# Exponents of a gated attention cell as fp32r products: Z in two parts instead of three, the mask's product first, rows of a parity on their own partitions

## The reference, cut to what matters

```python
ig, fg = gates(q, k, v)                      # 8 heads each
log_f = jax.nn.log_sigmoid(fg)
cs = jnp.cumsum(log_f, axis=1)
log_D = where(tril, cs[:, :, None] - cs[:, None, :], -inf) + ig[:, None, :]
max_log_D = jnp.max(log_D, axis=-1, keepdims=True)
D_mat = jnp.exp(log_D - max_log_D)
C = (qh @ kh.T / sqrt(32)) * D_mat
normalizer = maximum(abs(C.sum(-1)), exp(-max_log_D))
h = (C / (normalizer + 1e-6)) @ vh           # then a norm over 256 features, and x = x + h
```

## Time and profile before

| | |
|---|---|
| device time, 3 runs | median 572.49 us (571.02 to 572.50) |
| profiled execution | 568.18 us, span of the engines 566.5 us |
| PE busy | 547.5 us (97%) |
| DVE busy | 326.7 us (58%) |
| ACT busy | 230.2 us (41%) |
| stage A | about 25.2 to 118.7 us of the span |

### The profile page before, as it was taken

The page is one execution under the profiler, slowest core; times in us unless marked ns, Lnnn a source line. Parts: engine busy times, 40 slices in busy tenths (PEclk is TensorE's granted clock), DMA queues, the critical chain, the costliest instruction groups (busy, mean ns, idle before and its releaser), DMA issues.

```text
span 566.5 us, 8464 instructions
## 1 busy us (share of the span) xinstructions
PE 547.5 (97%) x2773; PEld 447.2 (79%) x2773; DVE 326.7 (58%) x799; ACT 230.2 (41%) x436; POOL 71.2 (13%) x105
## 2 busy tenths in 40 slices
PE   7798998999999999899999999999999999999997
PEld 5566576679888888778888878888878889788887
DVE  6677789768877779773353463434552444542333
ACT  2344545647878844362121361122351122441111
POOL 5232324111412323100000000000000000000000
PEclk9998999999999999999999999999999999999999
DMA  7685537334986999200000100000100000000001
GB/s 206 161 199 175 99 105 185 91 118 169 363 303 204 198 318 229 78 1 0 1 0 1 37 2 1 0 1 0 37 1 1 1 1 19 20 1 0 1 0 39
DMA packets 59296, 47.69 MB, mean 84 GB/s; under 512 B 37278, under 2 KB 50590, under 8 KB 58852
## 3 DMA queue, kind: packets, MB, share of 16 engines
q1 hardware_dynamic: 54264, 30.39, 20.1%
q0 software_dynamic: 4848, 16.78, 9.1%
q10 hardware_dynamic: 148, 0.04, 0.0%
HBM read 40.58 MB, written 2.10 MB: 75 GB/s over the span
## 4 chain that ended last, share of the span: by engine, by line
PE 58%; issue 7%; POOL 2%; DVE 1%; POOLq 0%; DVEq 0%
PE ps L914 57%; POOL rstd L445 1%; POOL h L551 1%; PE ps L584 0%; PE ps L878 0%; DVE qr L1527 0%; DVE x L1515 0%; DVE xn L1275 0%; DVE alT L1554 0%; DVE xT L1282 0%; POOL w L540 0%; POOLq L551 0%; POOL w L542 0%; PE ps L869 0%; DVE ot L1607 0%
## 5 line engine op out<-in xcount | busy, mean ns | idle before, releaser
L914 PE MATMUL ps<-hBt,h 128*128 128x512 f32 x512 | 117.5, 390 | 0.0
L914 PE MATMUL ps<-hA,h 128*128 128x512 f32 x512 | 117.3, 390 | 0.0
L1238 ACT ACTIVATE h<-ps,scol 128x512 f32<-128x512 f32 x64 | 44.2, 690 | 175.3 <-PE ps L914 175.2
L914 PEld LDWEIGHTS ps<-hA,h 128*128 128x128 f32 x512 | 95.9, 188 | 20.4 <-DVE hA L1581 0.6
L914 PEld LDWEIGHTS ps<-hBt,h 128*128 128x128 f32 x512 | 95.8, 188 | 20.3 <-DVE hBt L1581 0.6
L914 PE MATMUL ps<-xT,w 128*128 128x512 f32 x256 | 61.7, 396 | 1.0 <-DVE xT L1282 1.0
L914 PEld LDWEIGHTS ps<-xT,w 128*128 128x128 f32 x256 | 46.2, 188 | 15.0 <-issue 6.0
L1599 DVE CAST hBt<-h 128x512 fp32r<-128x512 f32 x32 | 13.7, 427 | 73.7 <-ACT h L1238 73.7
L1599 DVE CAST hA<-h 128x512 fp32r<-128x512 f32 x32 | 13.7, 427 | 70.0 <-ACT h L1238 70.0
L445 POOL TENSOR_TENSOR rstd<-ve,mhalf 128x4 f32<-128x4 f32 x16 | 16.7, 1041 | 262.9 <-DVE ve L1270 262.9
L1221 ACT ACTIVATE silD<-ps,scol 128x512 f32<-128x512 f32 x32 | 22.1, 689 | 45.2 <-PE ps L914 45.2
(11 more groups left out here) (174 smaller groups left out, 877.2 us busy)
## 6 DMA issues: line engine op xcount, KB each, us to landing
looked<-w_all_in SPq DMA_DIRECT2D x16, 704.0 KB, 5.6
h<-w_all_in POOLq DMA_DIRECT2D x16, 512.0 KB, 6.5
V<-ctx_in SPq DMA_DIRECT2D x32, 128.0 KB, 3.4
Qb<-xT SPq DMA_DIRECT2D x64, 64.0 KB, 2.1
w<-w_all_in POOLq DMA_DIRECT2D x3, 1024.0 KB, 7.7
x<-x_in SPq DMA_DIRECT2D x4, 512.0 KB, 4.2
kstA<-ctxT_in SPq DMA_DIRECT2D x4, 512.0 KB, 5.4
kstC<-ctxT_in SPq DMA_DIRECT2D x4, 512.0 KB, 5.8
```

The source lines that it names most:

```text
L914: last = mm(o, a, b, start=(k == 0 and p == 0), stop=(k == n_k - 1 and p == 1))
L1238: fn(h32[:, m % 2, :], ps[:, 2 + m % 4, :], ACT.Gelu, scale=scol[:, L + 1, m:m + 1])\
```

## The change

Z is split into two parts of fp32r in place of three of bf16. `gate_c` has two DVE operations for four, `move_rows` four DMAs for six (now of 4-byte elements, 16 KB instead of 8 KB each). `Rr` and `Lr` have 2 + 8 = 10 rows for 15; the rows of even groups lie on partitions 0 to 9, those of odd groups on partitions 32 to 41. The mask and the identity are fp32r as well; the mask is kept once (128 columns) and read four times over. In `expo` the mask's product comes first, then the rows' product. For the first batch of a group both mask products come before the wait for z_moved. A batch's two expo come one after the other, then its two qk. The ones rows and the mask are loaded by POOL (five DMAs that convert from bf16) and not by SP.

```diff
+ZP = 2
+RZ = ZP + ZP * Q
+RB = 32
-MOVES = 16 * 6
+MOVES = 16 * 2 * ZP
...
-        Rr = place(a3, "Rr", [RA, 2, Q, 2, Q, S], BF16)
-        Lr = place(a3, "Lr", [RA, 2, 2, Q, S], BF16)
+        Rr = place(a3, "Rr", [RB + RZ, Q, 2, Q, S], F32R)
+        Lr = place(a3, "Lr", [RB + RZ, 2, Q, S], F32R)
...
         def move_rows(sp, u):
-            for part in range(3):
-                sp.dma_start(Rr[part:part + 1, u, :, :, :, :], zp[:, part, 0, :]).then_inc(s["z_moved"], 16)
-                sp.dma_start(Lr[3 + part * Q:3 + part * Q + Q, u, :, :, :], zp[:, part, 1, :])\
-                    .then_inc(s["z_moved"], 16)
+            for part in range(ZP):
+                sp.dma_start(row_of(u, part), zp[:, part, 0, :].bitcast(F32)).then_inc(s["z_moved"], 16)
+                sp.dma_start(columns_of(u, part), zp[:, part, 1, :].bitcast(F32)).then_inc(s["z_moved"], 16)
...
+            def causal(quad):
+
+                mm(ps[:, EX + quad, :], idr[:, :], tri_all, start=True, stop=False)
+
             def expo(g, u, k):
                 q, quad = k // 2, k % 2
                 n = UN * g + k
                 if k == 0:
+                    for a in range(2):
+                        pe.wait_ge(s["d_ready"], n + a + 1)
+                        causal(a)
                     pe.wait_ge(s["z_moved"], MOVES * (g + 1))
-                    pe.wait_ge(s["d_ready"], n + 1)
-                mm(ps[:, EX + quad, :], Lr[:, u, quad, q, :], Rr[:, u, :, quad, q, :],
-                   start=True, stop=False)
-                mm(ps[:, EX + quad, :], idb[:, :], tri[:, :, :], start=False, stop=True)\
-                    .then_inc(s["expo_done"], 1)
+                elif k > 1:
+                    if quad == 1:
+                        pe.wait_ge(s["d_ready"], n + 1)
+                    causal(quad)
+                rows = slice(RB * u, RB * u + RZ)
+                mm(ps[:, EX + quad, :], Lr[rows, quad, q, :], Rr[rows, :, quad, q, :],
+                   start=False, stop=True).then_inc(s["expo_done"], 1)
...
-            pe.wait_ge(s["consts"], CONSTS)
+            pe.wait_ge(s["rows_ld"], ROWS)
...
                         for k in (2 * q, 2 * q + 1):
                             expo(g, u, k)
+                        for k in (2 * q, 2 * q + 1):
                             qk(g, u, k)
...
                 ch.step(v.tensor_copy(zp[:, 0, :, :], Z[:, :, :]))
                 ch.settle()
-                ch.step(v.tensor_tensor(zr[:, :, :], Z[:, :, :], zp[:, 0, :, :], ALU.subtract))
-                ch.settle()
-                ch.step(v.tensor_copy(zp[:, 1, :, :], zr[:, :, :]))
-                ch.settle()
-                v.tensor_tensor(zp[:, 2, :, :], zr[:, :, :], zp[:, 1, :, :], ALU.subtract).then_inc(s["z_ready"], 1)
+                v.tensor_tensor(zp[:, 1, :, :], Z[:, :, :], zp[:, 0, :, :], ALU.subtract).then_inc(s["z_ready"], 1)
```

More of the change, by code:

```diff
@@ L45 @@
 EPS = 1e-6
-CONSTS = 16 * 10
+A2 = 6
+CONSTS = 16 * 5
+ROWS = 16 * 5
 W_ALL = 2 * KD * HD + MD * D + 2 * MD * HD
@@ L128, in two_layers @@
         idf = place(base, "idf", [P, P], F32)
-        idb = place(base, "idb", [P, P], BF16)
-        tri = place(base, "tri", [P, Q, S], BF16)
+        idr = place(base, "idr", [P, P], F32R)
+        tri = place(base, "tri", [P, S], F32R)
         lns = place(base, "lns", [P, D], F32)
@@ L273, in _ @@
             sp.dma_start(gb[:, :], gb_in).then_inc(s["consts"], 16)
-            for u in range(2):
-                sp.dma_start(Rr[3:RA, u, :, :, :, :], ones_rows_in[3:RA]).then_inc(s["consts"], 16)
-                sp.dma_start(Lr[0:3, u, :, :, :], ones_rows_in[0:3, 0]).then_inc(s["consts"], 16)
-            sp.dma_start(tri[:, :, :], tri_in).then_inc(s["consts"], 16)
             sp.dma_start(x[:, Q:2 * Q, :], x_in[Q:2 * Q].rearrange("b s d -> s b d")).then_inc(s["x_second"], 16)
@@ L325, in _ @@
                     .then_inc(s["x_rest"], 16)
-            for part in range(3):
+            for part in range(ZP):
                 part_made(sp, part)
-                sp.dma_start(Rr[part:part + 1, 0, :, :, :, :], zp[:, part, 0, :]).then_inc(s["z_moved"], 16)
+                sp.dma_start(row_of(0, part), zp[:, part, 0, :].bitcast(F32)).then_inc(s["z_moved"], 16)
             queries_in(0, 0, 1)
@@ L460, in _ @@
                 .then_inc(s["gw_lo"], 1)
+            pool.dma_start(tri[:, :], tri_in[:, 0, :]).then_inc(s["rows_ld"], 16)
+            for u in range(2):
+                pool.dma_start(Rr[RB * u + ZP:RB * u + RZ, :, :, :, :], ones_rows_in[3:3 + ZP * Q]).then_inc(s["rows_ld"], 16)
+                pool.dma_start(Lr[RB * u:RB * u + ZP, :, :, :], ones_rows_in[0:ZP, 0]).then_inc(s["rows_ld"], 16)
             def k_lo(n, kst, u):
@@ L640, in qk @@
                 three(ps[:, QK + quad, :], lambda p: kT[:, u, p, quad, q * S:(q + 1) * S],
-                      lambda p: Qb[:, q % 2, p, quad, :, :], True, True,
-                      (lambda: pe.wait_ge(s["d_ready"], n + 2)) if quad == 0 else None).then_inc(s["qk_done"], 1)
+                      lambda p: Qb[:, q % 2, p, quad, :, :], True, True).then_inc(s["qk_done"], 1)
             def pv(b, par, nth, q, next_unit=None):
@@ L674, in _ @@
             pe.wait_ge(s["gw_lo"], 2)
-            pe.wait_ge(s["idb_ready"], 1)
+            pe.wait_ge(s["idr_ready"], 1)
             gates(0, 0, ctx_first=True)
@@ L1097, in _ @@
             floor_part(0)
-            for part in range(3):
+            for part in range(ZP):
                 part_made(act, part)
-                act.dma_start(Lr[3 + part * Q:3 + part * Q + Q, 0, :, :, :], zp[:, part, 1, :])\
-                    .then_inc(s["z_moved"], 16)
+                act.dma_start(columns_of(0, part), zp[:, part, 1, :].bitcast(F32)).then_inc(s["z_moved"], 16)
             with act.Fori(0, 2) as i:
```

42 lines of the change are left out of this document (24 added, 18 removed).

## The result

The changed kernel takes 576.83 us in the median of 6 runs (575.05 to 580.77), the kernel before 571.59 us (568.51 to 572.50, 6 runs): slower by the factor 1.0113, 95% interval 1.0068 to 1.0158. 570.0 us was forecast, with a range of 566.0 to 574.3. The profiled execution took 575.05 us, its span is 573.4 us (before 568.18 and 566.5).

A forecast was written before the change was run, and what follows sets the result against it. PE was taken to bound stage A, DVE close behind. Terms +5.3 - 4.8 - 2.9 - 0.6 = -3.0 us, taken as -2.5, gave 565.7 from the profiled 568.18; plus 4.3 for the median, 570.0 us, range 566.0 to 574.3.

The forecast's parts named there:

- the start's term: Start of stage A: the gate chain 0.7 us earlier, two masks before the wait; -0.6 us, bounds 0 and -1.1.
- the moves' term: Group starts in stage A: last move of Z leaves 1.9 us earlier, both stalls on moved rows go; -2.9 us.
- PE, +5.3 us: PE, 12 batches q = 1 to 3: four row changes with open fp32r loads, +0.44 us each batch; bounds 2.6 to 9.1.
- Rival B: PE in stage A: row changes cost no more than before, or less; about -6 us, 566.5 us; chance 0.07.
- DVE's stalls, -4.8 us: Stage A: all six PE stalls on DVE (`hm` and `Ct`) should go, -4.8 us.
- Rival E: Stage A: PE's lateness passes through DVE, the six stalls stay; +1.8 us, 574.3 us; chance 0.18.
- Late next is Qb, whose issues also move 1.9 us ahead: Group starts in stage A: `Qb` is the next late transfer, and its issues also come 1.9 us earlier.
- the bound "nothing": Moves of Z: the least gain allowed, nothing, if POOL's weights in the same queues rule the landing; otherwise all 2.9 us.
- The five new POOL issues ... stand in a gap of 5.31 us: Start: POOL's five new loads take at most 3.7 us, within a gap of 5.31 us before rstd.
- The prediction's own sign: Start of stage A: the prediction is wrong if `rows_ld` holds PE there; no size given.
- Rival C: Clock in stage A: stalls gone, one or both half-speed stretches go, 1.7 to 3.5 us more gain; 567.4 us; chance 0.16.
- The median against the profiled run, 4.3 us: Whole time: the three runs' median lay 4.3 us above the profiled execution; added to 565.7, giving 570.0 us.

The follow-up runs named there:

- e1: The changed kernel with ones rows and mask loaded as bf16 by SP and converted by ACT and POOL, replacing POOL's five converting loads: 571.19 us.
- e9: e1 with only 64 columns of stage B's raw weight copies loaded and summed, most of the weight check left out: 565.70 us.
- e10: The kernel before, with only 64 columns of stage B's raw weight copies loaded and summed, most of the weight check left out: 569.42 us.
- e2: The changed kernel with mask, mask, rows, rows at the start of every batch, not only a group's first: 578.44 us.
- e16: The changed kernel with only 64 columns of stage B's raw weight copies loaded and summed, most of the weight check left out: 570.32 us.
- e17: The changed kernel with 24 idle PE products in place of 10 ahead of the start's small transpose: 574.81 us.
- e5: e1 with the order of the kernel before: rows, mask, scores of one unit, then of the other: 578.20 us.
- e4: The kernel before with its rows' product padded with zeros from 15 to 128 partitions, ones rows loaded later: 570.93 us.

## Why the prediction was wrong, point by point

The step that failed first is the start's term: it was forecast at -0.6 us, and the first exponents came 2.7 us later. With POOL's loads gone (e1) the kernel takes 571.19 us, inside the stated range. The second is the moves' term of -2.9 us: a wait of 3.8 us on `Qb` took the place of the one on the rows. The terms of PE and DVE held.

- **PE, +5.3 us: right.** The loads after, in the third batch of the first group (PEld):

```profile
38.64 0.19 PEld L639 LDWEIGHTS ps<-tri,idr 128*128 128x128 f32 x1
39.08 0.18 PEld L654 LDWEIGHTS ps<-Rr,Lr 10*128 10x128 f32 x1 [0.25 <-issue]
39.51 0.19 PEld L639 LDWEIGHTS ps<-tri,idr 128*128 128x128 f32 x1 [0.25 <-issue]
39.94 0.18 PEld L654 LDWEIGHTS ps<-Rr,Lr 10*128 10x128 f32 x1 [0.25 <-issue]
40.37 0.19 PEld L604 LDWEIGHTS ps<-Qb,kT 128*128 128x128 f32 x1 [0.24 <-issue]
40.48 0.19 PEld L605 LDWEIGHTS ps<-Qb,kT 128*128 128x128 f32 x1
```

  Each change of rows stands at 0.43 us for 0.23, and a 10-row load takes 0.18 us, as long as one of 128. A batch of q > 0 takes 3.09 to 3.19 us, forecast 3.14. Rival B is refuted.
- **DVE's stalls, -4.8 us: right.** 3.8 us of brackets are 0.3 now, and e9's and e10's lists agree (0.3 and 2.9). Rival E (574.3 us, the nearest in time) had the wrong mechanism: PE's lateness did not pass through DVE.
- **The moves of Z, -2.9 us: wrong.** The stalls on the rows went as said (0.2 us is left). But "Late next is Qb, whose issues also move 1.9 us ahead" took an earlier issue for an earlier landing. They moved 1.1 us ahead (from the group's start; the last move of rows 0.6 us, not 1.9), into a burst that moved 1.4 us back, and PE waited 3.8 us for them. I had POOL's pieces in view only as a cause of the rows' stall; the bound "nothing" should have had a bound below nothing.
- **The start, -0.6 us: wrong, +2.7 us in the profile, and the largest single term: 5.6 us on the time (e1).** "The five new POOL issues ... stand in a gap of 5.31 us" is a sum over POOL's queue. Their price was on SP, whose four issues of `V` took 3.1 us longer. The sentence "SP loses five issues" counted what left SP's queue and not what the same bytes do from another. The prediction's own sign, that `rows_ld` holds PE at the start, came true in e2, e16 and e17, which start as the changed kernel does.
- **The clock, in no term of the sum.** Rival C had it as a gain, since the stalls would go; they moved, and up to 4 of the 5.2 us lost are stretches at half speed. In the second group the clock is 0.94, one stretch for two, but two stretches came elsewhere. A stall has to be priced with the stretch that may follow it (1.7 us), on both signs.
- **The median against the profiled run, 4.3 us:** most of the spread of one kernel's runs goes with the clock. Over the 35 runs of before, from 1.000 down to 0.990, a clock lower by 0.01 goes with 5 us more. That doesn't explain the profiled run: at 568.18 us it had a clock of 0.994, with which those 35 runs take 569.7 to 572.2 us. Its short tail (3.3 us) may be part of it. So 6.9 us between the two profiles stand against 5.2 us between the medians.

What stays open: why the raw copies can't be placed for nothing, how much of e9's gain is ACT's, how the start's 5.6 us are made up, why e5 loses 7 us, and what brings a half-speed stretch on after one wait and not after another.

## What to carry to other kernels

Before moving a transfer ahead, look at what the DMA engines carry at the new time: an earlier issue into a burst lands later. A load that goes from the sync engine to GpSimd is priced on the other queues' issues, not on GpSimd's own gap. And price each wait of PE with the half-speed stretch that can follow it; where transfers set the waits, work taken off PE may not show in the time at all (e2, e4).
